# A graph and feed-forward pipeline on one core: a new order of the first loads and of the first weight fold

## What is computed

```python
x = x + _L0_gnn_ref(_layernorm(x, axis=-1), adj, L0_gnn_W, L0_gnn_b)
x = x + _L0_ffn_ref(_layernorm(x, axis=-1), L0_ffn_weight, L0_ffn_bias)
x = x + _L1_gnn_ref(_layernorm(x, axis=-1), adj, L1_gnn_w_se, ...)
x = x + _L1_ffn_ref(_layernorm(x, axis=-1), L1_ffn_ln_w, L1_ffn_ln_b, L1_ffn_W, L1_ffn_b)
```

## Time and profile before

| | us |
|---|---|
| median of 3 runs | 1294.8 |
| lowest, highest | 1294.2, 1296.26 |
| the profiled execution | 1294.57 |
| its span | 1292.8 |

### The profile page before, as it was taken

One profiled execution on the slowest core, in us unless ns is written; L12 is line 12 of the kernel. 1 busy time (PEld: TensorE's weight loads), 2 busy tenths in 40 slices (PEclk: granted clock), 3 DMA queues, 4 the chain that ended last, 5 costly groups with the idle time before them and its releaser, 6 DMA issues.

```text
span 1292.8 us, 29543 instructions
## 1 busy us (share of the span) xinstructions
PE 1257.6 (97%) x9309; PEld 1122.5 (87%) x9309; DVE 1189.0 (92%) x2808; ACT 1005.8 (78%) x1410; POOL 960.8 (74%) x783
## 2 busy tenths in 40 slices
PE   8899999999999999689999999999999999999998
PEld 7677777777777777489999999999999999999998
DVE  7888888888888877799999999999999999999997
ACT  2455555555555555789999999999999999999995
POOL 3455555544555554489999999999999999999996
PEclk9999999999999999889999999999999999999999
DMA  6111111111111000000000000000000000000004
GB/s 192 42 42 42 49 52 54 48 41 41 41 41 41 0 1 1 1 2 0 0 0 0 0 0 0 0 0 0 0 0 0 0 0 0 0 0 0 0 0 130
DMA packets 29808, 27.71 MB, mean 21 GB/s; under 512 B 3285, under 2 KB 21464, under 8 KB 29656
## 3 DMA queue, kind: packets, MB, share of 16 engines
q1 hardware_dynamic: 29784, 27.41, 6.5%
HBM read 23.21 MB, written 4.19 MB: 21 GB/s over the span
## 4 chain that ended last, share of the span: by engine, by line
PE 83%; DVE 10%; ACT 3%; issue 3%; POOL 0%; DMA 0%; SPq 0%; DVEq 0%; ACTq 0%; POOLq 0%
PE psum L860 33%; PE psum L876 16%; PE psum L856 7%; PE psum L631 4%; PE psum L633 4%; PE psum L632 4%; PE psum L802 4%; PE psum L653 3%; PE psum L648 3%; DVE emb_n L1409 2%; DVE xh_mem L1233 1%; PE psum L642 1%; ACT emb_f L993 1%; PE psum L662 1%; DVE upd L1370 1%
## 5 line engine op out<-in xcount | busy, mean ns | idle before, releaser
L482 POOL TENSOR_TENSOR f_rs<-f_var,half_neg 128x8 f32<-128x8 f32 x240 | 395.1, 1646 | 24.5 <-DVE f_var L1299 5.4
L930 ACT ACTIVATE g_ring<-u_ring 128x1024 f32<-128x1024 f32 x240 | 407.1, 1696 | 3.1 <-DVE u_ring L1274 3.0
L953 ACT ACTIVATE y_all<-psum 128x1024 f32<-128x1024 f32 x240 | 397.2, 1655 | 8.7 <-PE psum L876 8.7
L860 PEld LDWEIGHTS psum<-w_t,y_all 128*128 128x128 f32 x2880 | 382.8, 193 | 9.4
L940 ACT ACTIVATE t_ring<-psum 128x1024 f32<-128x1024 f32 x232 | 388.1, 1673 | 3.0 <-PE psum L860 3.0
L860 PE MATMUL psum<-w_t,y_all 128*128 128x128 f32 x2880 | 388.6, 275 | 0.0
L1262 DVE BATCH_NORM_STATS2 f_stat<-g_ring 128x6 f32<-128x256 f32 x960 | 341.9, 418 | 3.5 <-ACT g_ring L930 3.5
L488 POOL TENSOR_TENSOR h_ring<-g_ring,f_rs 128x640 f32<-128x640 f32 x240 | 302.1, 1259 | 18.8
L1274 DVE SCALAR_TENSOR_TENSOR u_ring<-t_ring,psum 128x1024 f32<-128x1024 f32 x232 | 279.0, 1203 | 0.7 <-ACT t_ring L940 0.7
L876 PE MATMUL psum<-ident,h_ring 128*128 128x128 f32 (+1 forms) x1920 | 252.2, 275 | 2.4 <-issue 2.4
L947 ACT ACTIVATE h_ring<-g_ring,f_rs 128x128 f32<-128x128 f32 x240 | 248.3, 1035 | 1.6 <-POOL f_rs L482 1.6
(11 more groups left out here) (194 smaller groups left out, 2136.0 us busy)
## 6 DMA issues: line engine op xcount, KB each, us to landing
work<-in_adj_dram SPq DMA_DIRECT2D x16, 1024.0 KB, 5.4
x_tok<-in_x_dram SPq DMA_DIRECT2D x16, 256.0 KB, 5.6
out_dram<-y_all SPq DMA_DIRECT2D x7, 512.0 KB, 3.2
work<-in_L_gnn_conv_w_dram SPq DMA_DIRECT2D x1, 1088.0 KB
out_dram<-y_all SPq DMA_DIRECT2D x2, 256.0 KB, 3.5
work<-in_L_gnn_w_ih_dram SPq DMA_DIRECT2D x1, 384.0 KB
work<-in_L_gnn_w_hh_dram SPq DMA_DIRECT2D x1, 192.0 KB
work<-in_L_gnn_W_dram SPq DMA_DIRECT2D x1, 64.0 KB, 5.1
```

Of the source, the lines that this page charges most:

```text
L482: pool.tensor_tensor(f_rs[:, j % 4, :], f_var[:, j % 2, :], half_neg[:, 0:GT], ALU.pow).then_inc(f_pow, 1)
L860: m = pe.matmul(y_ps[k % 2][:, h, C * t:C * t + C], y_all[:, GT * k + NT * h + t, :], w1_t[:] if t < biased else w1c_t[:], start=False, st ...
L930: act.activation(g_ring[j], u_ring[j % 2], ACT.Silu).then_inc(f_silu, 1)
L953: act.activation(y_all[:, GT * j:GT * j + GT, :].rearrange("p t c -> p (t c)"), g_ps[j % 2].rearrange("p h n -> p (h n)"), ACT.Copy).then_ ...
```

## The change

It does five things.

1. SyncE issues x of graph 0 first, on a semaphore of its own (`s_x0`), and the adjacency of graph 0 second. Then come the two first weights and biases as before, W1 on a semaphore of its own (`s_w1`), the rows and columns, and only then the six other weights. `load(1, 1)` stays last.
2. VectorE waits for `s_x0` and runs `stats(0, 0)` ahead of `degree(0)`. It adds the 16 to `s_in[0]` itself. The first fold, now `fold_first`, stands behind `degree(0)`.
3. TensorE turns the two folded weights behind all four quarters of the adjacency of graph 0, ahead of the 7 `keep_awake` products. Ahead of `turn_weights(0, 4)` it now waits for `s_wload`.
4. ScalarE copies the two turned weights behind the two even quarters.
5. `fold()` waits for `s_small` and `s_w1`, no longer for all weights. GpSimd's wait for `s_wload` ahead of the tap sums stays, with six transfers to count instead of seven.

```diff
-        weights = [(nat[:, N_W1, :], w1), (conv2_nat, conv2_w),
+        weights = [(conv2_nat, conv2_w),
...
-            load(0, 0)
+            sp.dma_start(x_tok[:, graph(0), :], x_dram[0]).then_inc(s_x0, 16)
+            sp.dma_start(adj_in[0], adj_dram[0]).then_inc(s_in[0], 16)
             for dst, src in ((nat[:, N_W0, :], w0), (nat[:, N_WF, :], wf),
                              (bcol[:, B0:B0 + 1], col(b0)), (bcol[:, BF:BF + 1], col(bf))):
                 sp.dma_start(dst, src).then_inc(s_first, 16)
-            for dst, src in weights:
-                sp.dma_start(dst, src).then_inc(s_wload, 16)
+            sp.dma_start(nat[:, N_W1, :], w1).then_inc(s_w1, 16)
...
             sp.dma_start(emb_bias, b_se.rearrange("(o i) -> o i", o=1)).then_inc(s_small, 16)
+            for dst, src in weights:
+                sp.dma_start(dst, src).then_inc(s_wload, 16)
             load(1, 1)
...
             keep_awake(DIST_B, 20)
-            pe.wait_ge(s_folded0, 1)
-            for j in range(2):
-                m = pe.transpose(bank[CONV][:, C * j:C * j + C], nat[:, N_W0 + j, :], ident[:])
-            m.then_inc(s_wturn0, 1)
+
+            def turn_first():
+                pe.wait_ge(s_folded0, 1)
+                for j in range(2):
+                    m = pe.transpose(bank[CONV][:, C * j:C * j + C], nat[:, N_W0 + j, :], ident[:])
+                m.then_inc(s_wturn0, 1)
...
                     if b is None:
+                        turn_first()
                         keep_awake(DIST_B, 7)
...
                         spread_vectors()
+                        pe.wait_ge(s_wload, 16 * NWEIGHTS)
                         turn_weights(0, 4)
...
-            act.wait_ge(s_wturn0, 1)
-            act.activation(w_full[:, W0:W0 + 2, :], tiles(bank[CONV])[:, 0:2, :], ACT.Copy).then_inc(s_wfull, 1)
...
                 if l0:
+                    if b is None:
+                        act.wait_ge(s_wturn0, 1)
+                        act.activation(w_full[:, W0:W0 + 2, :], tiles(bank[CONV])[:, 0:2, :], ACT.Copy).then_inc(s_wfull, 1)
                     act.wait_ge(s_q, c + 1)
...
                 dve.wait_ge(s_small, 16 * NSMALL)
-                dve.wait_ge(s_wload, 16 * NWEIGHTS)
+                dve.wait_ge(s_w1, 16)
...
+                if ends(d, 0):
+
+                    dve.wait_ge(s_x0, 16)
+                    stats(0, 0)
+                    dve.sem_inc(s_in[0], 16)
                 if d is not None and (b is not None or not l0):
                     degree(d, p)
-                    if b is None:
-                        stats(0, d)
+                if ends(d, 0):
+                    fold_first()
```

More of the change, by code:

```diff
@@ L195, in build @@
         s_first = sem("s_first")
+        s_x0 = sem("s_x0")
+        s_w1 = sem("s_w1")
         s_small = sem("s_small")
@@ L1115, in _, with fold_first @@
             link(ins)
-            dve.wait_ge(s_first, 16 * 4)
-            first = nat[:, N_W0:N_W0 + 2, :]
-            link(dve.tensor_reduce(bcol[:, T0:T0 + 2], first, AX_X, ALU.add))
-            link(dve.tensor_tensor(bcol[:, U0:U0 + 2], bcol[:, B0:B0 + 2], bcol[:, T0:T0 + 2], ALU.subtract))
-            link(dve.tensor_scalar(bcol[:, T0:T0 + 2], bcol[:, U0:U0 + 2], 1.0 / C, None, ALU.mult))
-            dve.tensor_tensor(first, first, spread(bcol[:, T0:T0 + 2], 2, C), ALU.add).then_inc(s_folded0, 1)
+            def fold_first():
+                dve.wait_ge(s_first, 16 * 4)
+                first = nat[:, N_W0:N_W0 + 2, :]
+                link(dve.tensor_reduce(bcol[:, T0:T0 + 2], first, AX_X, ALU.add))
+                link(dve.tensor_tensor(bcol[:, U0:U0 + 2], bcol[:, B0:B0 + 2], bcol[:, T0:T0 + 2], ALU.subtract))
+                link(dve.tensor_scalar(bcol[:, T0:T0 + 2], bcol[:, U0:U0 + 2], 1.0 / C, None, ALU.mult))
+                dve.tensor_tensor(first, first, spread(bcol[:, T0:T0 + 2], 2, C), ALU.add).then_inc(s_folded0, 1)
             def fold():
```

## The result

| | us |
|---|---|
| median of 22 runs, changed kernel | 1297.34 (1294.97 to 1299.87) |
| median of 22 runs, kernel before, beside them | 1294.60 (1293.57 to 1296.26) |
| ratio | 1.0019, 95% interval 1.0013 to 1.0025 |
| the profiled execution (its span) | 1298.05 (1295.9) |

The change makes the kernel slower by 0.19%, 2.5 us by the ratio (the medians differ by 2.7). 2.6 us was taken as the least that can be told from no change, so it lies just inside; with 22 runs on each side the interval is clear of 1. The profiled execution is 3.5 us longer than that of before, more than the medians, and its span 3.1 us.

The account below looks back on a forecast made before the run. The opening, acting as a sum, was taken as the part reached, with graph 1's load the place to watch: -1.7 early, +2.9 waiting, +1.2 on 1294.57 gives 1295.8 us; own range 1294.6 to 1296.9, stated range 1294.0 to 1299.0.

Parts of the forecast that it names:

- The direction, and the place: Opening, VectorE's second row sums: they wait for graph 1's load behind 1.84 MB of weights; run slower by 1.2 us.
- The gain early on: VectorE in the opening: 2.25 + 0.7 - 1.2 = 1.75, taken as 1.7 us earlier up to graph 1's row sums.
- The landing: SP's queue: graph 1 lands at 13.7 + 6.3 + 1.84 / 0.337 = 25.5 us, 1.7 later than before.
- The bounds of 24.3 and 26.5: Graph 1's landing at 426 GB/s (shift of 0) and at 282 GB/s (shift of +2.3).
- loads are served in the order of issue: SP's queue: bytes ahead must move first, so graph 1 cannot overtake the weights; bytes counted from the weights' issue on.
- +2.9 waiting there: VectorE arrives at graph 1's row sums at 22.6 and stands until 25.5; with -1.7 this sums to +1.2 us.
- The step that failed: TensorE idles 2.7 us before graph 1's norm ends; clock falls after about 2.8, so only from a landing of about 25.6.
- the forecast's own range: Whole run, from the bounds of the queue's rate: 1294.6 to 1296.9 us, forecast chance 0.62.
- the prediction's signs of being wrong: VectorE's idle missing or under 1.7 us, weights after 23, opening clock under 1.00, or shift at 38 us unlike the end's.
- the clock case: Rival, chance 0.22: TensorE's clock falls in its wait, costing 2 to 3 us more; 1297.8 to 1299.6, say 1298.3.
- The early gain: Rival, chance 0.06: graph 1 lands by 22.6, the turn starts 1.7 us earlier, 1292.9.
- the tie: Rival, chance 0.10: queue runs at its fast end or a later wait swallows the shift, 1294.6 us.

Follow-up runs that it names:

- e_conv_ahead: Changed kernel with only the convolution weight ahead of graph 1's load, the other five weights behind it: 1293.95 us, ratio 0.9994; unedited again 1293.89, ratio 0.9989.
- e_load1_first: Changed kernel with the load of graph 1 issued ahead of the six long weights: 1299.26 us, ratio 1.0031 to the kernel before.
- e_engines_only: Changed kernel with its later loads back in the order of before, long weights ahead of rows and columns: 1295.54 us, ratio 1.0004 to the kernel before.
- e_conv_early: e_conv_ahead with the convolution weight moved between the rows and the columns: 1294.13 us, ratio 0.9994 to the kernel before.

## Why the prediction was right, and where it was not

**The direction, and the place.** Slower, at VectorE's second row sums, for want of graph 1's x behind 1.8 MB of weights: shown, by the idle time there released by a DMA in every kernel with this order of loads, and by its going when bytes were taken from ahead of the load.

**The gain early on.** 1.7 forecast, 1.85 measured at the first copy, 1.77 at VectorE's arrival in the first profile; sums at 7.01 (7.1 forecast), fold waiting until 14.81 (14.9). In the second profile of the same kernel only 0.7 of it reached the second row sums, because of the add beside GpSimd's tap sum. The prediction has no term for that.

**The landing.** 25.5 forecast; 26.00, 25.67, 25.27, 25.88 and 25.12 in the five profiles with the six weights ahead. The bounds of 24.3 and 26.5 held them all. The sum counts from the issue of the weights, 13.7 forecast and 13.56 measured, so the way from there took 12.4 us instead of 11.8. The rate was not what was off: from 14 to 26 us the queue moved a mean of 327 GB/s, near the 337 that were taken. That is 3.9 MB, while the six weights and graph 1 have 3.15. The other 0.8 MB must be load 2's, the only other load in the queue then, issued at 18.30 and 19.20, behind graph 1. So "loads are served in the order of issue" holds for who lands first, and not for the bytes: the last of graph 1 shares the queue with what stands behind it, and bytes behind a load belong in the sum too. The weights landed at 21.1, as GpSimd's start shows below, 21.6 forecast:

```profile
21.06 1.74 POOL L528 TENSOR_TENSOR conv_pre<-work 128x512 f32<-128x512 f32 x1 [10.12 <-DMA work<-in_L_gnn_w_se_dram]
```

The term "+2.9 waiting there" was thus 3.5 in the profiled execution, and the sum +1.7 instead of +1.2.

**The step that failed** is the one that left the fall of the clock out of the forecast: "So it decides at a landing of about 25.6, just beyond my 25.5". Two things were wrong in it. First, the 0.1 us between the two numbers could not carry the odds of 0.62 to 0.22, since the landing's own bounds lay 2.2 us apart. It came at 26.00 and 25.88 in the two profiles of the changed kernel, TensorE idled for 3.48 and 3.35 us instead of 2.7, and by the prediction's own point the fall was then due; it is in both. Second, there is no such point. It was read from one wait of 1.40 us that held and one in which the fall came after 2.8. The runs show a fall 1.7 us into a wait, falls behind waits of 1.52, 1.53 and 1.70 us, and one with no wait above 0.93 us close before it, while the clock held over 1.56 us in the changed kernel (at 39.22 above) and over 1.51 and 1.52 us in the kernel before. So the length of one wait does not decide it; what does is not shown here. The Trainium skill, TensorE: Matmul & The Clock Gate, section on why this matters for kernels, warns of idle gaps between bursts of matmuls. The trace agrees as far as the longer gaps go: the clock fell behind each of the three open ones of 3.35 to 3.56 us.

The forecast therefore had the cheaper half of what happens: +1.2 against a measured 2.5 to 2.7. The median of 1297.34 lies above the forecast's own range, which ended at 1296.9, and one of the prediction's signs of being wrong, a clock under 1.00 in the opening, came true. The median lies inside the stated range of 1294.0 to 1299.0 only because that took in most of the clock case. Direction and place were foreseen; that the number held is owed to the width. The case's price was too high in turn: 2 to 3 us forecast, 1.4 to 1.7 measured, because the clock came back after 3.4 us and not 4 to 6. Late load and fall together are 3.4 in the profiled execution, inside the 3.2 to 4.2 of that case; over many runs, 1294.97 to 1299.87, the time lies between the forecast and the case.

**The rivals.** The early gain did not stand, and the tie did not come; a version where it partly does exists (`e_conv_ahead`). The shift at the third row sums, 3.39, is nearly that of the span, 3.1, so the opening does act as a sum.

**What stays open:** which share of the executions loses the clock in the changed kernel, how the median divides between the late load and the clock, and why the kernel before spreads over 2.7 us. One thing that changes from execution to execution is when the adjacency of graph 0 lands: its row sums start between 6.8 and 7.2 in eight profiles with x issued first, and at 8.2 and 8.5 in two others.

## What to carry to other kernels

Moving a load back in a queue moves everything behind it back too: add up the bytes ahead of each later load and compare the landing with the moment its first reader arrives, not with the one whose wait is being removed. Add some of the bytes behind it as well, since they moved alongside here. A gain that one engine makes ahead of such a load turns into waiting there, and on TensorE that waiting can cost a second time through the clock. Work that waits for the moved bytes, like GpSimd's tap sums here, moves too and can land on another engine's critical operations. Here what helped was to send ahead of the next input only the bytes that are read before it.

## What the runs showed of the hardware

- TensorE's granted clock fell to its lower level behind waits of 1.52, 1.53 and 1.70 us in some executions, 1.7 us into a wait in `e_load1_first`, and once, near 22.7 in `e_engines_only`, with no wait above 0.93 us in the ten us before. It held its upper level over waits of 1.51, 1.52 and 1.56 us in others.
- Loads issued later moved bytes before an earlier one had landed: 3.9 MB from 14 to 26 us in the changed kernel, where the loads up to graph 1 had 3.15.
- The issue of a column of 0.5 KB on SP took 0.43 us when the queue had little to move and up to 1.05 us while 1.1 MB were moving.
- Short loads issued from ScalarE did not wait for SP's longer ones: beside 19 of them the first 1.3 MB landed at 10.6 us, against 7.0 in most executions and 8.5 in the latest without them.
- Some VectorE operations, each reading two tensors in SBUF, took longer beside GpSimd's tap sums on 128x512: 0.93 and 1.30 us instead of 0.29 in `e_conv_early`, and 1.54 to 1.75 us instead of 0.69 in three other profiles.
